# Adding 38 unread fp16 products a turn to TensorE in an LSTM's recurrence

## What is computed

```python
def step(carry, xs):
    h, c = carry
    xi_t, xf_t, xg_t, xo_t = xs
    i_t = jax.nn.sigmoid(xi_t + h @ V_i)
    f_t = jax.nn.sigmoid(xf_t + h @ V_f)
    g_t = jnp.tanh(xg_t + h @ V_c)
    o_t = jax.nn.sigmoid(xo_t + h @ V_o)
    c_new = h * c + i_t * g_t
    h_new = o_t * jnp.tanh(c_new)
    return ((h_new, c_new), h_new)
```

## Time and profile before

| what | value |
|---|---|
| median of three runs | 1247.31 us (1242.23 to 1248.82) |
| the profiled execution | 1245.91 us |
| its span in the profile | 1243.8 us |
| instructions | 24449 |
| PE, DVE, ACT, POOL busy | 83%, 69%, 43%, 20% of the span |
| mean granted TensorE clock | 0.778 of full speed |
| first and last h1 of the recurrence | 440.10 us and 843.73 us, 256 steps |

### The profile page before, as it was taken

The page is one execution under the profiler, slowest core; times in us unless marked ns, Lnnn a source line. Parts: engine busy times, 40 slices in busy tenths (PEclk is TensorE's granted clock), DMA queues, the critical chain, the costliest instruction groups (busy, mean ns, idle before and its releaser), DMA issues. The chain is left out here.

```text
span 1243.8 us, 24449 instructions
## 1 busy us (share of the span) xinstructions
PE 1034.0 (83%) x8081; PEld 591.4 (48%) x8081; DVE 858.6 (69%) x2869; ACT 533.9 (43%) x1414; POOL 244.4 (20%) x319
## 2 busy tenths in 40 slices
PE   6878886867899778888888888868928999999996
PEld 2456652253577655555555556545413333333332
DVE  7786845855575566767666766764485888888885
ACT  3644543544344334343433444335515454544542
POOL 4604012300010000000000000000001565655555
PEclk9988887978899955555555555557968999999998
DMA  7000002000000000000000000000007555554640
GB/s 247 1 1 2 1 2 85 1 1 1 3 1 1 1 1 1 0 0 0 0 0 0 0 0 0 0 3 1 1 0 181 117 120 127 123 133 110 144 111 9
DMA packets 11256, 47.57 MB, mean 38 GB/s; under 512 B 1841, under 2 KB 6321, under 8 KB 6705
## 3 DMA queue, kind: packets, MB, share of 16 engines
q1 hardware_dynamic: 11184, 46.62, 15.4%
HBM read 43.99 MB, written 2.62 MB: 37 GB/s over the span
## 5 line engine op out<-in xcount | busy, mean ns | idle before, releaser
L2372 ACT ACTIVATE ex_gated<-wide,unscale 128x1024 f32<-128x1024 f32 x128 | 142.2, 1114 | 139.9 <-PE wide L2338 139.8
L2388 DVE TENSOR_TENSOR ex_hid<-wide,ex_gated 128x1024 f32<-128x1024 f32 x128 | 156.0, 1223 | 39.1 <-ACT ex_gated L2372 26.7
L2314 POOL TENSOR_TENSOR ex_acc<-ex_part,ex_acc 128x512 f32<-128x512 f32 x120 | 152.7, 1272 | 94.7 <-DVE ex_part L2404 80.3
L1839 ACT ACTIVATE terms<-wide 128x32 f32<-128x32 f32 x256 | 54.7, 214 | 165.5 <-PE wide L1743 161.7
L1739 PE MATMUL wide<-h,vh 128*128 128x16 f16 x768 | 63.7, 181 | 73.0 <-DVE h L1929 71.6
L1739 PEld LDWEIGHTS wide<-h,vh 128*128 128x128 f16 x768 | 40.6, 109 | 162.3 <-DVE h L1929 162.3
L2350 PE MATMUL wide<-ex_hid,w 128*64 128x512 f32 x512 | 116.7, 598 | 0.0
L2202 POOL TENSOR_TENSOR ro_en<-ro_e,ro_top 128x1024 f32<-128x1024 f32 x1 | 2.7, 2712 | 574.8 <-DVE ro_top L2238 574.8
L1920 DVE TENSOR_TENSOR_SCAN cells<-terms 128x48 f32<-128x48 f32 x256 | 66.1, 258 | 57.8 <-ACT terms L1839 49.5
L2338 PE MATMUL wide<-xh,wh 64*128 64x512 f16 x512 | 99.2, 384 | 5.1 <-PEq L83 3.7
L2338 PE MATMUL wide<-xh,wl 64*128 64x512 f16 x512 | 98.5, 381 | 0.0
(11 more groups left out here) (402 smaller groups left out, 2113.4 us busy)
## 6 DMA issues: line engine op xcount, KB each, us to landing
ex_d<-route SPq DMA_DIRECT2D x64, 512.0 KB, 6.4
par_attn<-in_attn SPq DMA_DIRECT2D x1, 2704.0 KB, 13.1
par_rest<-in_rest SPq DMA_DIRECT2D x1, 2523.5 KB, 18.5
L_xin<-in_x SPq DMA_DIRECT2D x8, 256.0 KB, 5.8
w<-in_w SPq DMA_DIRECT2D x1, 2048.0 KB, 8.1
out<-ex_acc SPq DMA_DIRECT2D x16, 128.0 KB, 3.5
w<-in_w SPq DMA_DIRECT2D x1, 512.0 KB, 9.0
route<-ro_dt SPq DMA_DIRECT2D x2, 256.0 KB, 2.0
```

What stands on the lines that cost most here:

```text
L1839: act.activation(two_gates, bank[b][:, 2 * q * HB:2 * (q + 1) * HB].rearrange("p (g b) -> p g b", g=2), ACT.Tanh, scale=back).then_inc(s[" ...
L2314: pool.tensor_tensor(acc[:, t % 2, :], part[:, (e // 2) % 2, e % 2, :], acc[:, t % 2, :] if e else tile_of(m.xa, t), ALU.add)\
L2372: act.activation(gated[:, n % 2, :], pair_of_up(n // GS, 2 * (n % GS))[:], ACT.Silu, scale=m.unscale[:, 0:1]).then_inc(s["gated_ready"], 1)
L2388: dve.tensor_tensor(hid[:, n % (2 * GS), :], pair_of_up(n // GS, 2 * (n % GS) + 1)[:], gated[:, n % 2, :], ALU.mult).then_inc(s["hid_ready ...
```

## The change

After the work beside the chain, PE makes further products in every step of every turn: `vh` of the first gate (128 x 128, fp16) by all of `vh` (384 columns), into bank 5, which nothing reads. Their number depends on k and is 38 for a turn, 608 for all turns. The layer norms' sums move from bank 5 to bank 7, beside the queries, in columns 256 to 263. As the sums and the queries now share a bank, PE waits ahead of the sums until ACT has taken the queries of the turn before; ACT raises that semaphore once more at the start, so that the counts fit. Nothing else changes.

```diff
         def sums(n):
-            return bank[5][:, 4 * n:4 * n + 4]
+            return bank[7][:, 2 * P + 4 * n:2 * P + 4 * n + 4]
...
+            EXTRA = (2, 2, 3, 3, 2, 1, 3, 3, 2, 3, 4, 2, 4, 1, 3, 2)
+            flat_vh = vh[:].rearrange("p g n -> p (g n)")
+
+            def extra(n):
+                for _ in range(n):
+                    pe.matmul(bank[5][:, 0:3 * P], vh[:, 0, :], flat_vh, start=True, stop=True, skip_group_check=True)
...
                     if k == 2 and not last:
+                        if not first:
+                            pe.wait_ge(s["q_ready"], i)
                         sums_in(i + 1)
                     if k == 3 and not first:
+                        if last:
+                            pe.wait_ge(s["q_ready"], i)
                         sums_out(i - 1)
...
                     if k == 15 and not first:
                         queries(i - 1)
+                    extra(EXTRA[k])
...
             centre_out(TURNS - 1)
+            pe.wait_ge(s["q_ready"], TURNS)
             sums_out(TURNS - 1)
...
+            act.sem_inc(s["q_ready"], 1)
...
-                    ins = dve.tensor_scalar(v, bank[5][:, of], 1e-5, None, ALU.add)
+                    ins = dve.tensor_scalar(v, bank[7][:, 2 * P:2 * P + 8][:, of], 1e-5, None, ALU.add)
```

## The result

The changed kernel takes 1272.4 us (median of 4 runs, 1271.2 to 1275.1) against 1248.1 us (now four runs too): slower. The ratio is 1.0207 with a 95% interval of 1.0180 to 1.0234, which leaves open whether it is more than 2%. That is over the range of the prediction, and its sign is that of the first rival. The profiled execution took 1275.1 us, its span is 1273.0 us.

The account below looks back on a forecast made before the run. The prediction took the recurrence's chain, mostly DVE and ACT, to bound the kernel. Gains of 10.2 and 0.5 us, less 3.9 us for stretches at 1.2 GHz, gave 1247.3 - 6.8 = 1240.5 us, range 1230 to 1264.

Parts of the forecast that it names:

- the first rival: Recurrence: clock rises but falls every turn at k = 2 and 3, back four or five steps later; 1260 to 1266 us, chance 0.26.
- What bounds the kernel: Recurrence: a chain of 1.58 us a step, 0.26 us of it on PE, the rest on DVE and ACT.
- The parts at no cost: Moved sums cost nothing, the wait for the queries at most 0.4 us a turn; PE's queue has room for 608 instructions.
- The clock rises in the fullest steps, from 10 on: Recurrence, first turn: steps 10 to 15 and 0, 1 stream enough for PE to be granted the full clock.
- Once up ... more like the stretch that held at 416 us: Recurrence at 2.4 GHz: 28,160 of about 59,000 cycles a turn hold the clock, as PE busy 2.33 of 4 us did.
- The overrun at 1.2 GHz: Steps whose further products outlast PE's room of 1.28 us: 4.75 us a turn, 76 us in 16 turns if the clock stayed low.
- The price of the clock, 0.04 us a step: PE's 0.26 us of the chain gets 0.04 us shorter at 2.4 GHz: 256 steps, 10.2 us.
- the one-column rows: Products of 363 ns at 1.2 and 246 ns at 2.4 GHz; less the fp32 load, 10 ns a step, 2.6 us in all.

Follow-up runs that it names:

- the first experiment: The changed kernel without its further products, keeping the moved sums and the new wait: 1247.0 us, ratio 0.9999 to the kernel before.
- the fifth: The changed kernel with bias products of 128 rows, plus more further products where the clock was still lost: 1241.5 us, ratio 0.9963 to the kernel before.

## Why the prediction was wrong

- **What bounds the kernel**: right. The chain did, and the products could only delay it or shorten its one piece on PE.
- **The parts at no cost**: right. Moved sums and wait are worth nothing, by the first experiment; more instructions in PE's queue are not either, by the fifth, which has the most (25,913 against 24,449) and is the fastest.
- **The clock rises in the fullest steps, from 10 on**: right, it does so by steps 11 to 13 in nearly every turn.
- **"Once up ... more like the stretch that held at 416 us"**: this is the step that failed. I counted columns times passes, 28,160 cycles a turn (28,928 with 40 products), and in them the bias products of k = 4, 6, 8 and 9 as if they were like any other, 3,072 of the cycles. They have three rows. The second and third experiment show that such products do not keep the clock up: with three rows in all further products the clock never rose, with 128 in the bias products it held. So the thin place was not k = 2 and 3 alone but went on into k = 4 and 5, and the way back up was barred by k = 6, 8 and 9. The stretch at 416 us had products of 128 rows only; the comparison left out the one thing that differed.
- **The first rival**: the right course of events, with 0.26, and the sums as half of the cause. The place was one pair of steps too early, and the way back longer: seven steps at 1.2 GHz, half of the turn's time, not four or five. Its price, 19 us, was near the 24 measured, in part by luck: other steps overran than it said (1.9 us in a full turn, not 1.6), and its gain of 7.4 us was 2 (137 steps of 14 ns).
- **The overrun at 1.2 GHz**: near, where the changed kernel shows it (in the first turn and the slow halves). The steps behind k = 2, 7, 10 and 11 came 0.47, 0.23, 0 and 0.23 us late, where I had 0.52, 0.30, 0 and 0.28. Those behind bias products came later than I had it, 0.54 us for k = 4 and 8 and 0.44 for 6 and 9 against 0.41 and 0.30: the sum had no term for the change in the number of rows ahead of them and behind them. Over these eight steps I had 2.5 us, and 2.9 were measured.
- **The price of the clock, 0.04 us a step**: mis-sized by a factor of three. From the last three products to the tanh it is 14 ns: the second product starts 39 ns after the first in place of 48, and its own time is 169 ns in place of 174. The products of 512 columns lose 41 ns beyond their streaming, but a product of 16 columns does not lose that; the one-column rows, which I took as the lower end, were the nearer ones at 10. With the true price, held from the first step, the gain is 4 us, so even a clock that held could hardly have brought the 6.8 us that I forecast. By the Trainium skill, "TensorE: Matmul & The Clock Gate", section Single matmul latency, an estimate for 16 columns is 23 ns a step (24 in the prediction, from rounded values); measured are 14.

## What to carry to other kernels

Work that is there only to raise the clock has to be counted by the rows as well as the columns that it puts through the array, stretch by stretch: here the thinnest places of a turn decided, and that PE was shown busy in them told nothing of it. Before spending on the clock, price it on the chain: of a chain that waits on DVE, ACT and hand-overs, only 14 of 1580 ns were the clock's. And such work costs twice when the clock is lost, since it is then longer itself and stands in PE's queue ahead of the chain. An experiment that changes the rows of a product changes its time too, so look at the steps before taking its total for a price.

## What the hardware showed that I had not expected

Further products of three rows left TensorE at 1.2 GHz though PE was shown busy 511 of 513 us, while 125 more rows in the bias products, all of them zeros, were enough for the clock to hold in most turns. Whether rows between 3 and 128 count in part, no run here shows; the products of 64 rows, behind which the clock rose at 945 us in the kernel before, go two at a time. And a change in the number of rows holds PE up: at 1.2 GHz the step behind k = 7 took 2.04 us with further products of three rows and 1.81 with 128.

The fall at 587.2 us came after two steps in which PE was shown busy for 3.11 of 3.20 us:

```profile
584.00:587.20 3.20, 3.11 (x31) 1.78 (x31) 2.12 (x16) 1.06 (x8) 0.00 (x0) 0.99 0.00 0
```

The Trainium skill, "TensorE: Matmul & The Clock Gate", section What's actually happening, lays the fall to an idle stretch; the trace shows that PE need not be shown idle for it, nor have a pause as long as a step. And small products hardly feel the clock: with 16 columns, 14 ns of some 250.
